# A two-batch block of attention and experts: batch 0's second norm and routing moved among the attention pairs, and the last pair's denominators summed by TensorE

## The reference

```python
mod = silu(c) @ wmod                      # six vectors of 128 per batch: sa, ca, ga, sb, cb, gb
h = layernorm(x) * (1 + ca) + sa
x = x + ga * attention(h)                 # own layernorm, latents of 64, 16 heads of 64, rotary, softmax, residual
h = layernorm(x) * (1 + cb) + sb          # "the second norm"
x = x + gb * experts(h)

# attention, per head
scores = q @ k.T * scale ; attn = softmax(scores) ; out = concat(attn @ v) @ w_out.T + residual

# experts
scores = softmax(h @ gate_w + gate_b)     # 8 experts
top 2 of each token; for i in range(8):   # the last selected expert, by number, wins
    y = relu((h * w_i) @ w1[i] + b1[i]) @ w2[i] + b2[i]
    out = where(w_i > 0, y, out)
```

## Time and profile before

| | us |
|---|---|
| median of 3 runs | 899.38 (898.97 to 901.64) |
| the profiled execution | 900.41 |
| its span, first to last instruction | 898.7 |
| TensorE matmuls busy | 807.5 (90%) |
| GpSimd busy | 664.6 (74%) |
| VectorE busy | 633.1 (70%) |
| ScalarE busy | 391.1 (44%) |
| mean granted clock of TensorE | 0.947 of 2.4 GHz |

### The profile page before, as it was taken

The page is one execution under the profiler, slowest core; times in us unless marked ns, Lnnn a source line. Parts: engine busy times, 40 slices in busy tenths (PEclk is TensorE's granted clock), DMA queues, the critical chain, the costliest instruction groups (busy, mean ns, idle before and its releaser), DMA issues.

```text
span 898.7 us, 14641 instructions
## 1 busy us (share of the span) xinstructions
PE 807.5 (90%) x5118; PEld 484.9 (54%) x5118; DVE 633.1 (70%) x1141; ACT 391.1 (44%) x635; POOL 664.6 (74%) x348
## 2 busy tenths in 40 slices
PE   4779999999999999999999999999997967677771
PEld 2535555555555555555655555655553533377671
DVE  8987777778787878777777787777776548634122
ACT  3554444444444444444444444444543233254340
POOL 2579998999997979797978787878778545623213
PEclk8969999999999999999999999999999888979886
DMA  9100010101010101010110101010101000186872
GB/s 242 33 1 13 13 37 2 37 1 36 3 36 2 36 2 37 2 36 6 32 25 13 26 13 25 13 27 1 25 1 25 1 2 24 59 268 220 264 232 80
DMA packets 84089, 43.90 MB, mean 49 GB/s; under 512 B 57392, under 2 KB 73136, under 8 KB 83952
## 3 DMA queue, kind: packets, MB, share of 16 engines
q1 hardware_dynamic: 82992, 40.86, 17.8%
q0 software_dynamic: 1024, 2.10, 0.8%
HBM read 36.51 MB, written 6.16 MB: 47 GB/s over the span
## 4 chain that ended last, share of the span: by engine, by line
PE 80%; DVE 8%; DMA 4%; issue 3%; POOL 2%; ACT 1%; SPq 1%; POOLq 0%; DVEq 0%
PE ps_o L467 25%; PE ps_m L432 9%; PE ps_x L420 8%; PE ps_s L451 6%; PE ps_s L457 6%; PE ps_s L453 6%; PE ps_s L455 6%; PE ps_s L494 4%; PE ps_s L605 2%; DMA moe<-xs_dram 2%; PE ps_s L476 2%; PE ps_s L614 2%; DVE mx L1114 1%; DVE hn L1205 1%; POOL xs_dram L970 1%
## 5 line engine op out<-in xcount | busy, mean ns | idle before, releaser
L956 POOL TENSOR_TENSOR acc<-acc,probs 128x1024 f32<-128x1024 f32 (+1 forms) x192 | 462.7, 2410 | 107.4 <-ACT probs L716 86.5
L1114 DVE TENSOR_REDUCE mx<-ps_m 128x2 f32<-128x1024 f32 x240 | 293.8, 1224 | 105.2 <-PE ps_m L432 104.7
L716 ACT ACTIVATE probs<-ps_s 128x1024 f32<-128x1024 f32 x256 | 248.9, 1024 | 162.1 <-PE ps_s L457 161.9
L467 PE MATMUL ps_o<-probs,c_all 128*64 128x512 f32 x1024 | 251.6, 613 | 0.0
L432 PE MATMUL ps_m<-k_hi,q_hi 64*128 64x512 f32 x480 | 107.7, 444 | 8.1 <-DVE mx L1114 8.1
L467 PEld LDWEIGHTS ps_o<-probs,c_all 128*64 128x64 f32 x1024 | 62.9, 137 | 95.2 <-issue 45.5
L451 PE MATMUL ps_s<-q_hi,k_hi 64*128 64x512 f32 x512 | 102.0, 394 | 1.3 <-ACT probs L716 1.2
L453 PE MATMUL ps_s<-q_hi,k_lo 64*128 64x512 f32 x512 | 100.9, 389 | 0.0
L457 PE MATMUL ps_s<-neg_row,one_row 64*128 64x512 f32 x512 | 100.9, 389 | 0.0
L455 PE MATMUL ps_s<-q_lo,k_hi 64*128 64x512 f32 x512 | 100.6, 388 | 0.0
L432 PEld LDWEIGHTS ps_m<-k_hi,q_hi 64*128 64x128 f32 x480 | 46.5, 184 | 94.1 <-issue 83.3
(11 more groups left out here) (299 smaller groups left out, 1001.1 us busy)
## 6 DMA issues: line engine op xcount, KB each, us to landing
probs<-in_experts SPq DMA_DIRECT2D x15, 578.0 KB
rr<-rd_dram SPq DMA_DIRECT2D x62, 128.0 KB
wu<-in_wqk SPq DMA_DIRECT2D x16, 256.0 KB, 2.6
neg_row<-nm SPq DMA_DIRECT2D x256, 0.5 KB, 2.0
w_first<-in_experts SPq DMA_DIRECT2D x5, 578.0 KB
rot<-in_experts SPq DMA_DIRECT2D x5, 578.0 KB
hT<-in_experts SPq DMA_DIRECT2D x5, 578.0 KB
xs_dram<-zero SPq DMA_DIRECT2D x2, 960.0 KB, 9.8
```

The lines of the kernel that those rows point to most:

```text
L467: ins = nc.tensor.matmul(ps_o[64 * h:64 * h + 64, :], c_all[:, (p // HP) * TB + kt, :], probs[:, st % 4, h, :], start=(kt == 0), stop=(kt ...
L716: nc.scalar.activation(probs[:, st % 4, :, :], ps_s[:, 2 * (st % 2):2 * (st % 2) + 2, :], ACT.Exp, scale=SCALE).then_inc(s["probs"], 1)
L956: V.tensor_tensor(acc[:, buf(p, half), heads, :], first, probs[:, st % 4, heads, :], ALU.add).then_inc(s["added"], 1)
L1114: V.reduce_max(mx[:, :, kh, qt], max_banks(q, n), AX.X).then_inc(s["max_reduced"], 1)
```

## The change

- Batch 0's statistics are taken in groups 2 and 4 of pair 9 and aggregated in group 6 (VectorE). Their inverse roots and shifts are computed on GpSimd at the start of pair 10 (four steps); ScalarE normalises two tiles in each of groups 3 to 6 of pair 10; GpSimd multiplies and adds the modulation at the start of pairs 11 and 12, one pass of 128x1024 each.
- TensorE transposes them behind the scores of groups 1 and 2 of pair 14, into `ps_x`, and makes the logits in group 3. VectorE's `judge`, `choose`, `scaled` and `find_slots` for batch 0 stand at the start of pair 15, behind its last maxima; ScalarE's exponential of the logits in group 0; TensorE's counts in group 3.
- In pair 15 GpSimd and VectorE add no probabilities. TensorE sums them itself, for each two steps with four products with 32 columns of ones, accumulated over a half in `ps_m` (`den_steps`). Pair 14's denominators move to group 1, both its outputs to group 5 (the second in `ps_x`).
- The last pair's denominators are brought onto the partitions by four small products each half (`den_columns`, with `head_row`, a new constant of five memsets), and inverted there (`recip_last`, 128x8). Its latent sums aren't divided: the outputs are made for each head by itself, 64 rows each, into two banks (`last_outputs`), and VectorE adds them to x with the head's inverse as scalar, eight steps of 128x128 per half (`out_add_last`). The first half's outputs stand in group 6.
- Batch 1's second norm is done by halves; its transposes come behind tiles 0 and 2, its logits behind tile 3, its counts behind tile 7. Batch 0's `scatter` follows the last add of pair 14 in GpSimd's list, then both inverse roots and batch 1's `scatter`.
- b2 of batch 0's tiles is added by TensorE, a product with one row. Of the six weight buffers two are now in `acc` and two in `probs`, none in `hT`; SyncE's waits for them change accordingly.

```diff
-        wb = ([w_first[:], flat(rot[:])[:, 0:WROW]] + [p_flat[:, n * WROW:(n + 1) * WROW] for n in range(3)]
-              + [hT[:, 0:WROW]])
+        wb = ([w_first[:], flat(rot[:])[:, 0:WROW]]
+              + [acc[:].rearrange("p b h n -> p (b h n)")[:, n * WROW:(n + 1) * WROW] for n in range(2)]
+              + [p_flat[:, n * WROW:(n + 1) * WROW] for n in range(2)])
...
-        T_H2, T_CN = 6, 9
+        T_FEAT, T_LOG, T_CN = (0, 2), 3, 7
+        last_banks = [(ps_m[:, 0, :], ps_x[:]), (ps_x[:], ps_m[:, 1, :])]
...
+            def den_steps(st):
+                half, kt = divmod(st, TB)
+                for n in range(2):
+                    for h in range(2):
+                        ins = nc.tensor.matmul(ps_m[quarter(2 * h + n), half, :], ones[:, 0:32], probs[:, (st + n) % 4, h, :],
+                                               start=(kt == 0), stop=(kt == TB - 2))
+                if kt == TB - 2:
+                    ins.then_inc(s["den_product"], 1)
+
+            def den_columns(half):
+                pe.wait_ge(s["den_read"], n_den(LAST, half))
+                ge(pe, s["out_added"], n_part(LAST, 0) if half else 0)
+                for n in range(4):
+                    ins = nc.tensor.matmul(ps_m[:, 0, 2 * n:2 * n + 2], den[:, n * P:(n + 1) * P], head_row[:],
+                                           start=True, stop=True)
+                ins.then_inc(s["den_columns"], 1)
+
+            def last_outputs(half):
+                pe.wait_ge(s["sums_copied"], n_part(LAST, half))
+                if half == 0:
+                    pe.wait_ge(s["inverses"], n_den(LAST, 0))
+                pe.wait_ge(s["out_added"], n_part(LAST, half) - 1)
+                for n in range(4):
+                    for h in range(2):
+                        ins = nc.tensor.matmul(last_banks[half][h][:, n * P:(n + 1) * P],
+                                               ou[rows(h), buf(LAST, half), n * P:(n + 1) * P],
+                                               g_all[rows(h), LAST // HP, LAST % HP, :], start=True, stop=True)
+                ins.then_inc(s["out_product"], 1)
...
-                    if p == LAST:
-                        if g == 0:
-                            pe.wait_ge(s["max_reduced"], NMAX * NPAIR)
-                            h2_features(0)
-                        if g == 1:
-                            logits(0)
-                        if g == 4:
-                            counts_before(0)
+                    if p == LAST - 1:
+                        if g in (1, 2):
+                            h2_features(0, g - 1)
+                        if g == 3:
+                            logits(0)
+                    if p == LAST and g == 1:
+                        pe.wait_ge(s["max_reduced"], NMAX * NPAIR)
+                    if p == LAST and g > 0:
+                        pe.wait_ge(s["probs"], n_step(p, 2 * g - 1))
+                        den_steps(2 * g - 2)
...
+                    if p == LAST:
+                        if g == 3:
+                            counts_before(0)
+                        if g in (1, 5):
+                            pe.wait_ge(s["probs"], n_step(p, 2 * g + 1))
+                        if g == 1:
+                            denominators(p - 1, ps_s[:, 2, :])
+                        if g == 5:
+                            outputs(p - 1, 0, ps_s[:, 3, :])
+                            outputs(p - 1, 1, ps_x[:])
+                            den_columns(0)
+                        if g == 6:
+                            last_outputs(0)
...
+            pe.wait_ge(s["probs"], NSTEP * NPAIR)
+            den_steps(NSTEP - 2)
             pv(LAST, NSTEP - 2)
             pv(LAST, NSTEP - 1)
+            den_columns(1)
...
+                if k < NA * GS:
+                    ins = nc.tensor.matmul(ps_s[:, 3, 0:D], ones_sq[0:1, :], b2_sb[i][0:1, :], start=False, stop=True)
...
+            def out_add_last(half):
+                dve.wait_ge(s["out_product"], n_part(LAST, half))
+                dve.wait_ge(s["inverses"], n_den(LAST, half))
+                for h in range(2):
+                    for n in range(4):
+                        xt = x_sb[:, TB + 4 * half + n, :]
+                        ins = V.scalar_tensor_tensor(out=xt, in0=last_banks[half][h][:, n * P:(n + 1) * P],
+                                                     scalar=rc_col[:, half, 2 * n + h:2 * n + h + 1], in1=xt,
+                                                     op0=ALU.mult, op1=ALU.add)
...
+                    if p == HP + 1:
+                        if g in (2, 4):
+                            block_stats(T0[2 * g - 4:2 * g])
+                        if g == 6:
+                            block_norm(T0)
             p = LAST
+            judge(0)
+            choose(0)
+            recip(p - 1)
+            scaled(0)
+            find_slots(0)
+            divide(p - 1, 0)
+            divide(p - 1, 1)
+            out_add(p - 1, 0, ps_s[:, 3, :])
+            out_add(p - 1, 1, ps_x[:])
+            recip_last(0)
             for half in range(2):
-                out_add(p, half, ps_x[:])
-                dve.wait_ge(s["out_added"], n_part(p, half))
+                out_add_last(half)
                 block_stats(T1[4 * half:4 * half + 4])
-            block_norm(1)
-            block_out(1)
+                block_norm(T1[4 * half:4 * half + 4])
+                block_out(half)
+                if half == 0:
+                    recip_last(1)
```

More of the change, by code:

```diff
@@ L215, in build @@
             "added": "a step is in the sums of probabilities (gpsimd)",
-            "added_last": "the same for head 1 of the last pair's second half (vector)",
             "den_product": "a pair's denominators; half of the last pair's (tensor)",
-            "den_read": "and read (scalar, the last half vector)",
+            "den_read": "and read (scalar)",
+            "den_columns": "half of the last pair's, queries on partitions (tensor)",
             "inverses": "denominators inverted (vector)",
@@ L223, in build @@
             "out_added": "and added to x (vector)",
-            "var2_ready": "variances after the attention (vector)",
-            "inv2_ready": "their inverse roots (gpsimd)",
-            "norm2": "a batch's second block input (vector)",
+            "var2_ready": "variances of batch 0's sums, then of batch 1's by halves (vector)",
+            "inv2_step": "a step of batch 0's inverse roots (gpsimd)",
+            "inv2_ready": "the inverse roots, batch 0's with their shifts (gpsimd)",
+            "norm2_rows": "batch 0's sums normalised (scalar)",
+            "norm2_scaled": "and scaled (gpsimd)",
+            "norm2": "second block input: batch 0's (gpsimd), then batch 1's by halves (vector)",
             "norm2_T": "half of it transposed (tensor)",
@@ L614, in down_e @@
                     ins = nc.tensor.matmul(ps_s[:, 3, 0:D], hid[i % 2][:, c * P:(c + 1) * P],
-                                           w2_sb[i][:, c * P:(c + 1) * P], start=(c == 0), stop=(c == 3))
+                                           w2_sb[i][:, c * P:(c + 1) * P], start=(c == 0), stop=(c == 3 and k >= NA * GS))
+                if k < NA * GS:
+                    ins = nc.tensor.matmul(ps_s[:, 3, 0:D], ones_sq[0:1, :], b2_sb[i][0:1, :], start=False, stop=True)
                 ins.then_inc(s["y_product"], 1)
@@ L770, in _, with h2_rows, h2T_out @@
             values_out(1)
-            def h2T_out(b):
-                for g in range(2):
-                    act.wait_ge(s["norm2_T"], 2 * b + g + 1)
-                    nc.scalar.copy(h2T[:, g * HALF:(g + 1) * HALF], ps_m[:, g, :]).then_inc(s["norm2_features"], 1)
+            def h2_rows(tiles):
+                act.wait_ge(s["inv2_ready"], 1)
+                for k in tiles:
+                    ins = nc.scalar.activation(h2[:, k, :], x_sb[:, k, :], ACT.Identity, bias=shift[:, k:k + 1],
+                                               scale=sd[:, 0, k:k + 1])
+                ins.then_inc(s["norm2_rows"], 1)
+            def h2T_out(b, g):
+                act.wait_ge(s["norm2_T"], 2 * b + g + 1)
+                nc.scalar.copy(h2T[:, g * HALF:(g + 1) * HALF], ps_m[:, g, :] if b else ps_x[:]).then_inc(s["norm2_features"], 1)
             def exp_logits(b):
@@ L796, in _ @@
                         o_out(p, 0)
-                    if p == LAST:
-                        if g == 0:
-                            h2T_out(0)
-                        if g == 1:
-                            exp_logits(0)
+                    if p == HP + 2 and g in (3, 4, 5, 6):
+                        h2_rows(range(2 * g - 6, 2 * g - 4))
+                    if p == LAST - 1 and g in (1, 2):
+                        h2T_out(0, g - 1)
+                    if p == LAST and g == 0:
+                        exp_logits(0)
+            den_out(LAST, ps_m[:, 1, :], 1)
+            o_out(LAST, 1)
             def hidden(i, k):
@@ L971, in scatter @@
```

(11 more changed lines are left out.)

244 lines of the change are left out of this document (109 added, 135 removed).

## The result

The changed kernel takes 868.89 us (median of 4 runs, 867.37 to 869.11) beside 899.99 for the kernel before: ratio 0.9651, 95% interval 0.963 to 0.9672, so 31 us less. The forecast was 865 (865.3 before rounding), with 857 to 873 as the range of 8 in 10. The profiled execution took 867.37 us with a span of 865.6 (forecast 866.3 and 864.6).

What follows compares the result with a forecast made beforehand. TensorE fills the steady pairs but stops in the last two; behind them one chain of batch 1 holds the end. Pairs end 759.8, first load 798.9, plus tiles 46.0, results 19.2, start 0.5: span 864.6, forecast 865, range 857 to 873.

Steps and rivals of the forecast that it cites:

- Pairs 9 to 13: Batch 0's second norm, moved into these pairs, costs 0 us; 0 to 3 taken into the range.
- Start: Five more memsets on VectorE delay the silu of c by 0.2 to 1.0 us, taken as 0.5.
- Pair 14: Group 1 at 675.9 to pair 15's group 1 at 715.7; stops of 5.90 and 7.28 go, GpSimd's adds just behind.
- Transposes and the clock: Pair 14's eight transposes take 1.07 us at the high clock; by the skill's rule pair 14 would be 0.9 longer.
- Pair 15: The rest of pair 15 takes 44.1 us from 715.7, so the pairs end at 759.8 against 777.6.
- No new stop in the pairs: In pair 15 the 5.30 us stop goes: counts are there at 730.5, TensorE asks at 731.6.
- Batch 1's chain: Behind the pairs, norm ready after 10.6 us instead of 29.4; then logits 775.6, counts 782.2, slots 786.9, first load 798.9.
- a product with one row for b2, two instructions, 0.2 to 0.3: In batch 0's tiles, this added product takes a tile from 1.9 to 2.1 us.
- the two are level, and I let the tiles start where the load does: Tiles 8 to 14 end at 799.3, batch 1's first load comes at 798.9; its tiles take 46.0 us from there.
- Results: Behind batch 1's last tile at 844.9, results take 19.2 us, to 864.1.
- tiles keep their length: Transfers, not batch 1's routing, set the experts' part, so only its start moves: 868.7 of span, 870; chance 0.17.

Runs made afterwards that it cites:

- the run with GpSimd's sums: Changed kernel with the last pair's probabilities summed by GpSimd again and denominators by one product a half: 888.36 us, ratio 0.9849.
- The product's run: Changed kernel with b2 in batch 0's tiles added by a 128-row product with the identity instead of the one-row product: 865.14 us, ratio 0.9609.
- the cut loads: Changed kernel with expert transfers for tiles 6 to 14 of batch 0 cut to 16 of 1156 columns: 868.79 us, ratio 0.9644.
- one group of three kernels: Changed kernel with identity product and held-back gathers, with scatters and gathers spread, and with identity product and spread gathers: 856.18, 863.28 and 854.77 us.

## Why the prediction was right, and where it was not

The forecast's span is 1.0 us off, by terms that cancel in part.

- **Pairs 9 to 13: right.** 43.41 to 43.51 us each; the cover of the norm cost at most 0.1 us (forecast 0, 0 to 3).
- **Start: wrong sign, small.** First denominators at 110.06 us against 110.97; forecast 0.5 later. Starts differ by more than this between runs of one code (first tile at 757.5 to 762.6 in kernels that are the same up to there), so the memsets' price isn't shown.
- **Pair 14: right.** From group 1 (675.10) to pair 15's group 1 (715.26) 40.2 us, forecast 39.8, both stops gone, GpSimd's adds just behind as said. Alone, the norm's move is worth 15.6 us of the kernel before and 16 of the changed one, more than its two stops: the low clock behind them goes as well.
- **Transposes and the clock: right.** Four take 0.66 at 677.59, and the stretch has a clock of 1.00. The Trainium skill's rule that transposes don't open the clock (TensorE: Matmul & The Clock Gate, Part 4) isn't touched by that: among other matmuls it was open, and nothing was lost.
- **Pair 15: right, 1.6 us too long.** Group 1 to the end took 42.5 us for 44.1. The sums delay by 1.00 as said, the head outputs run side by side (1.1, not 1.7).
- **No new stop in the pairs: right.** Counts were ready at 721.4 (forecast by 730.5) and asked for at 731.0; the choice of experts took 5.2 us without adds beside it, and 18 us of the whole hang on that and on the early scatter, as the run with GpSimd's sums shows.
- **Batch 1's chain: right, a little long.** 767.56 - 757.77 = 9.8 us from the pairs' end to the norm (forecast 10.6): adds 2.3 (2.1), power 1.0 (1.67), on half the columns. Logits end at 772.5 (775.6), counts 778.8 (782.2), slots 785.3 (786.9). First load 798.70, forecast 798.9: there the scatter and its landing took 13.4 for 12.0.
- **The step that failed: "a product with one row for b2, two instructions, 0.2 to 0.3", and with it "the two are level, and I let the tiles start where the load does".** The product costs 0.6 of a tile's 2.50 against 1.90 in batch 1, and I counted no stop there, though the trace before had stops of 1.02 and 3.81 us beside a series of indirect transfers, and the change put another series (the scatter) among the tiles. From the logits' end to tile 15's start TensorE needed 807.4 - 772.5 = 34.9 us, not 23.7: 11 tiles by 0.4 is 4.4, stops of 2.0 and 2.7, and 2.2 of low clock. So batch 0's tiles, not the load, held batch 1's: first load to last tile is 49.1 us where I had carried over 46.0. From the load to the first product of a tile it was 8.7 us, and 4.6 before (the row below); from there to the last product 40.4 for 41.4. The product's run gives back 4.9 us and so shows its share; the stops' share is read from the trace, and their cause is open.

```profile
838.04 1.91 PE L605 MATMUL ps_s<-moe,probs 128*128 128x128 f32 x8
```

- **Results: 17.8 for 19.2**, 1.4 less.
- **Rival "tiles keep their length":** its mechanism, the transfers, is refuted by the cut loads, but its warning was sound: the tile's work and not the routing was the bound. 

Together: tiles end 2.9 us late (847.8 for 844.9), the start's 0.5 didn't come, the results gave 1.4 back, and the span is 865.6 for 864.6. That the error is only 1.0 us is in part luck. Of the 11.2 us by which batch 0's tiles were too short in the sum, 3.1 were covered because the logits ended earlier (772.5 for 775.6). Another 4.2 were covered because the 46.0 hold 4.6 from load to first product, so that they put batch 1's first product at 803.5, with TensorE free at 799.3. Only 3.9 came through, and 1.0 of them was given back by batch 1's tiles.

## What to carry to other kernels

A stop of 5 us on TensorE in a full stretch costs more than its length, since the work behind it starts at the low clock: price it with both. When a chain behind a stage is shortened by 20 us, sum again what was hidden in its shadow, every product of it: here 0.4 us per tile became 5 us of the total. And take small two-input steps of VectorE away from GpSimd's long passes before counting on either.

## What the hardware showed that I had not expected

A product with one row between products of 128 rows is not cheap: 0.48 us for two instructions against 0.39 with 128 rows. From its start to the next group's start it is 0.41 for 0.23, and the groups ahead of it and behind it take 0.1 more each, 0.38 a tile in all. And beside GpSimd's series of eight indirect transfers TensorE, ScalarE and SyncE stood still together, for 1.0 to 3.4 us at a time beside the scatters and up to 5.2 beside the gathers, while GpSimd went on, and no semaphore explains it. The chain of waits of the changed kernel (start, us, what) gives the stretch to no engine,

```profile
790.87 2.24 another core or an unknown queue
793.16 4.27 another core or an unknown queue
```

and in the ten profiles that have these stops the first began 5.5 us (in two 4.4) behind batch 1's first scatter. Transfers at half the rate leave it as it is. Loading of code isn't it either: the two queues that carry instructions moved nothing in the changed kernel from 786 to 803. In one group of three kernels they were absent; their cause is not settled.
